# Attention over 4096 tokens: half of the q and k projections moved into the head loop, and context normalised per eight heads

## The reference

```
q, k, v = xn @ q_w.T + q_b, xn @ k_w.T + k_b, xn @ v_w.T + v_b     # 16 heads of 16 columns
attn    = softmax(q @ k.T / 4)                                     # 4096 x 4096 for each head
ctx     = attn @ v ;  attention = ctx @ out_w.T + out_b
ffn     = fp8(xn) @ fp8(weight).T, scaled back, + bias, rounded to bfloat16
```

## Time and profile before

| | us |
|---|---|
| median of 3 runs | 1857.53 (1855.82 to 1859.31) |
| the profiled execution | 1860.13 |
| its span, first to last instruction | 1858.3 |
| ACT busy | 1734.8 (93%), 1912 instructions |
| PE busy | 1639.0 (88%), 33418 matmuls |
| DVE busy | 1637.7 (88%), 1923 instructions |
| POOL busy | 45.9 (2%) |
| DMA, 57.19 MB | 10.3% of 16 engines on the main queue |
| mean granted clock of PE | 0.997 |

### The profile page before, as it was taken

One profiled execution on the slowest core, in us unless ns is written; L12 is line 12 of the kernel. 1 busy time (PEld: TensorE's weight loads), 2 busy tenths in 40 slices (PEclk: granted clock), 3 DMA queues, 4 the chain that ended last, 5 costly groups with the idle time before them and its releaser, 6 DMA issues.

```text
span 1858.3 us, 74491 instructions
## 1 busy us (share of the span) xinstructions
PE 1639.0 (88%) x33418; PEld 553.2 (30%) x33418; DVE 1637.7 (88%) x1923; ACT 1734.8 (93%) x1912; POOL 45.9 (2%) x57
## 2 busy tenths in 40 slices
PE   6998888888888888888888888888888888888888
PEld 4632222222222222222222222222222222222226
DVE  8688989989898998989898998989899898989896
ACT  2379999999999999999999999999999999999990
POOL 0000000000000000000000000000000000000003
PEclk9999999999999999999999999999999999999999
DMA  6430100000010000001010000101000010001003
GB/s 189 163 99 10 32 8 18 20 19 24 10 32 10 24 12 18 24 16 26 10 32 8 16 22 19 24 10 32 10 24 11 18 24 17 26 10 32 8 14 108
DMA packets 94965, 57.19 MB, mean 31 GB/s; under 512 B 55280, under 2 KB 87280, under 8 KB 94640
## 3 DMA queue, kind: packets, MB, share of 16 engines
q1 hardware_dynamic: 94160, 52.18, 10.3%
q10 hardware_dynamic: 480, 0.20, 0.0%
HBM read 30.54 MB, written 17.30 MB: 26 GB/s over the span
## 4 chain that ended last, share of the span: by engine, by line
ACT 44%; issue 31%; PE 15%; DVE 7%; POOL 1%; ACTq 1%; DMA 0%; SPq 0%; POOLq 0%; DVEq 0%
ACT probs L683 44%; PE banks L1312 7%; PE banks L1271 4%; PE banks L1168 3%; DVE bits L988 2%; DVE d_probs L1006 2%; PE banks L1179 1%; DVE o_sb L966 1%; DVE o_junk L967 1%; ACTq L682 1%; POOL o_sb L604 0%; POOL o_junk L604 0%; DMA qk_bias<-in_L_attn_k_b_dram 0%; DVE xn_all L837 0%; PE banks L1152 0%
## 5 line engine op out<-in xcount | busy, mean ns | idle before, releaser
L683 ACT ACTIVATE probs<-banks 128x1024 f32<-128x1024 f32 x1856 | 1701.6, 1165 | 1.7 <-PE banks L1271 1.5
L1312 PE MATMUL banks<-probs,v_st 64*32 64x512 f32 x14848 | 972.2, 590 | 3.6
L1271 PE MATMUL banks<-q_st,k_st 50*32 50x512 f16 x16384 | 782.1, 381 | 193.3 <-ACT probs L683 171.1
L1271 PEld LDWEIGHTS banks<-q_st,k_st 50*32 50x32 f16 x16384 | 230.8, 89 | 1124.1 <-ACT probs L683 1003.2
L1312 PEld LDWEIGHTS banks<-probs,v_st 64*32 64x32 f32 x14848 | 263.3, 106 | 67.9 <-DVE o_junk L967 12.8
L988 DVE TENSOR_SCALAR bits<-banks 128x1024 int32<-128x1024 f32 x192 | 233.9, 1218 | 32.7 <-PE banks L1271 29.4
L995 DVE SCALAR_TENSOR_TENSOR horner<-powers 128x1024 f32<-128x1024 int32 x192 | 235.3, 1226 | 6.6
L1001 DVE SCALAR_TENSOR_TENSOR horner<-powers,horner 128x1024 f32<-128x1024 f32 x192 | 235.2, 1225 | 6.6
L1006 DVE SCALAR_TENSOR_TENSOR d_probs<-horner,bits 128x1024 int32<-128x1024 f32 x192 | 235.2, 1225 | 6.6
L998 DVE SCALAR_TENSOR_TENSOR powers<-powers,horner 128x1024 f32<-128x1024 int32 x192 | 235.1, 1225 | 6.6
L992 DVE TENSOR_SCALAR powers<-bits 128x1024 int32<-128x1024 int32 x192 | 133.2, 694 | 6.6
(11 more groups left out here) (102 smaller groups left out, 418.9 us busy)
## 6 DMA issues: line engine op xcount, KB each, us to landing
k_st<-k_parts SPq DMA_DIRECT2D x102, 64.0 KB, 2.2
q_st<-q_parts SPq DMA_DIRECT2D x198, 32.0 KB, 1.9
k_st<-k_parts SPq DMA_DIRECT2D x102, 60.0 KB, 2.2
q_st<-neg_row SPq DMA_DIRECT2D x264, 1.0 KB, 1.7
xnT_copy<-probs SPq DMA_DIRECT2D x8, 512.0 KB, 3.1
q_parts<-x8T SPq DMA_DIRECT2D x16, 256.0 KB, 2.9
k_parts<-x8T SPq DMA_DIRECT2D x16, 256.0 KB, 2.4
w_f<-xnT_copy SPq DMA_DIRECT2D x16, 256.0 KB, 3.0
```

What stands on the lines that cost most here:

```text
L683: act.activation(probs[:, at:at + WIDE * CHUNK].rearrange("p (t c) -> p t c", t=WIDE), banks[:, bank:bank + WIDE, :], ACT.Exp, bias=EXP_SHIFT,
L1271: last = pe.matmul(banks[cols, bank + g, :], k_st[rows, keys], blocks[rows, j], start=True, stop=True, tile_position=(g * GROUP, t * VCOLS))
L1312: last = pe.matmul(banks[VCOLS * qb:VCOLS * (qb + 1), 6 + half, cols], v_st[keys, kt, :], src[keys, g * CHUNK:(g + 1) * CHUNK][:, cols], s ...
```

## The change

**Ahead of the loop** the second round of projections is gone. The weights for heads 8-15 are copied aside by ACT into `late_w`. SP saves the turned chunk ahead of the parts. The first maximum comes directly behind the last chunk's q and k, and v of the last chunk behind that. Three of the four maxima of x (2048 columns each) go into the first loop; scaling and quantising the ffn weight move to the end of unit 0. A constant headroom now comes out of a filled row of q_st, so that `minus_maxima` has one instruction less.

**Units of heads 0-7** get two additional places (33 and 63 of 67), where PE projects 256 columns of q or k of heads 8-15. DVE takes the result in two instructions (`late_part`), SP saves it in four transfers a unit and loads 256 KB of turned x twice a unit. The places of DVE's blocks and of the maximum differ there: `LATE_D_AT`, `LATE_MAX_AT`.

**Taking sums.** DVE no longer turns and normalises: it adds the two banks into ctx_out by a copy and an addition, and the context is saved as it is. SP also saves the denominators, in four more transfers of 16 pieces of 128 bytes. After eight heads SP loads all their denominators, DVE takes reciprocals of 128x128 numbers for each u, SP saves those and loads them again, each spread over 16 partitions by one of eight transfers. DVE multiplies the context by them in sixteen parts of 128x512 (`scale_context`): parts 0 to 7 in units 17 to 24 (counted from 0; the last unit is 31) behind the block at place 29, parts 8 and 9 behind the last sums, parts 10 to 15 within output groups 0 to 5, each ahead of the group's last addition. SP's loads for 12 to 15 stand between the saves of output groups 0 to 3.

```diff
-    D_AT = (8, 17, 29, 37, 46, 55)
-    MAX_AT = 25
+    D_AT = (8, 17, 29, 37, 46, 55)
+    MAX_AT = 25
+    LATE_D_AT = ((4, 13, 25, 37, 45, 55), (4, 13, 25, 36, 45, 54))
+    LATE_MAX_AT = 21
+    LATE_AT = (33, 63)
+    LATE_UNITS = 16
...
+                self.layouts = [Layout(D_AT)] if full else [
+                    [Layout(LATE_D_AT[u], LATE_MAX_AT, LATE_AT) for u in range(UNITS)],
+                    [Layout(D_AT, MAX_AT) for u in range(UNITS)]]
...
             def save_context(c, h, u):
...
+                    if not c.full:
+                        to = den_dram[k, u, row:row + 1, :].rearrange("o (t x) -> o t x", x=P)[:, :, cols]
+                        sp.dma_start(to, ctx_out[u][qb * VCOLS + DH:qb * VCOLS + DH + 1, :].rearrange(
+                            "v (t x) -> v t x", x=VCOLS)).then_inc(ctx_saved[u], 16)
...
-            save_second(0)
+            for n in range(NCH - 1):
+                save_turned(n)
+                save_parts(n, (0, 1))
             sp.wait_ge(fills, FILLS)
+            sp.wait_ge(parts_saved[buffer_of(1, 0)], SAVED_0 + 32 * (NCH // 2))
             load_k(first, 0, 2)
-            save_second(1)
-            save_second(2)
             load_k(first, 0, 0)
-            save_second(3)
-            save_second(4)
+            save_turned(NCH - 1)
+            save_parts(NCH - 1, (0, 1))
             load_rows(first, 0, 1)
...
+            def share_reciprocals(i):
+
+                k, u, part = i // (UNITS * QB), i // QB % UNITS, i % QB
+                sp.wait_ge(rden_saved, 16 * (k * UNITS + u + 1 if k else UNITS))
+                if i >= 2:
+                    sp.wait_ge(ctx_scaled, i - 1)
+                src = rden_dram[k, u][:, part * CHUNK:(part + 1) * CHUNK]
+                for g in range(HEADS // KD):
+                    sp.dma_start(rden_rows[g * DH:(g + 1) * DH, i % 2, :], src[g, :].partition_broadcast(DH)
+                                 ).then_inc(rden_in[i % 2], 16)
...
                     save_context(c, h, 1)
+                    if not c.full and h == HEADS - 1:
+                        load_dens(1, 1)
+                        for i in scales_loaded(HEADS, 0):
+                            share_reciprocals(i)
...
+                    if not again and i == 0:
+                        save_reciprocals(1, 1)
+                    if not again and i < QB:
+                        share_reciprocals(SCALES - QB + i)
...
+            def scale_context(i):
+
+                k, u, part = i // (UNITS * QB), i // QB % UNITS, i % QB
+                dve.wait_ge(rden_in[i % 2], 16 * (HEADS // KD) * (i // 2 + 1))
+                dve.wait_ge(ctx_saved[u], (k + 1) * (HEADS // KD) * 2 * SAVES)
+                rows = ctxT[:, k, u, part * CT:(part + 1) * CT, :]
+                dve.tensor_tensor(rows, rows, rden_rows[:, i % 2, :].rearrange("p (t x) -> p t x", x=P), ALU.mult
+                                  ).then_inc(ctx_scaled, 1)
...
+                def late_part(h, u, slot):
...
+                    dve.tensor_scalar(buf[:, 0, :], src, qk_bias[:, o, 1:2], None, ALU.add).then_inc(late_hi, 1)
+                    dve.wait_ge(late_hi, i + 1)
+                    dve.scalar_tensor_tensor(out=buf[:, 1, :], in0=src, scalar=qk_bias[:, o, 1:2], in1=buf[:, 0, :],
+                                             op0=ALU.add, op1=ALU.subtract).then_inc(late_ready, 1)
...
-                    chain(dve.transpose(o_sb[:, :], banks[:, 6, :]), link0 + 1)
-                    dve.transpose(o_junk[:, :], banks[:, 7, :]).then_inc(c.acc_free, 1)
...
+                    chain(dve.tensor_copy(o_sb[:, :], banks[:, 6, :]), link0 + 1)
+                    dve.scalar_tensor_tensor(out=ctx_out[u][:, :], in0=banks[:, 7, :], scalar=1.0, in1=o_sb[:, :],
+                                             op0=ALU.mult, op1=ALU.add, accum_out=o_inf[:, span(h * 2 + u, 1)]
+                                             ).then_inc(c.ctx_ready, 1)
...
+                            d_block(h, u, lay.d_at.index(p))
+                            if n == FIRST_SCALED - 1 and p == lay.d_at[1]:
+                                reciprocals(0, 0)
+                                reciprocals(0, 1)
+                            if n == HEADS * UNITS - 1 and p == lay.d_at[2]:
+                                reciprocals(1, 0)
+                            if 0 <= n - FIRST_SCALED < SCALES // KD and p == lay.d_at[2]:
+                                scale_context(n - FIRST_SCALED)
...
+                    if not again and i < GROUPS_OUT - 2:
+                        scale_context(SCALES - GROUPS_OUT + 2 + i)
+                    if not again and i == 0:
+                        reciprocals(1, 1)
                     for b in range(2):
                         dve.wait_ge(proj_done, n * 2 + (b + 1))
...
+                def late_projection(h, u, p, slot):
...
+                    for k in range(KD):
+                        x_cols = late_x[:, slot, k, :]
+                        last = pe.matmul(banks[:, bank_at(h, u, p), 0:LATE_COLS], late_w[:, o, k, :],
+                                         x_cols if o else x_cols.rearrange("f (i j p) -> f j i p", i=CT // 2, j=QB),
+                                         start=(k == 0), stop=(k == KD - 1))
```

More of the change, by code:

```diff
@@ L282, in __init__ @@
[L282 to L286, removed]
-                self.a_index = {p: a for a, p in enumerate(self.a_places)}
-                self.takes = [p for p in range(self.places) if p not in self.a_index]
-                self.head_takes = UNITS * len(self.takes)
@@ L297, in __init__ @@
-                self.sum_at = {kt: at for at, kt in enumerate(self.sum_rows)}
-                self.summed = [1 + max(self.sum_at[kt] for kt in range(half * (KT // 2), (half + 1) * (KT // 2)))
-                               for half in range(2)]
-                left = [(at, None) for at in range(KT)]
-                self.sums_at = {}
-                p = SUMS_FROM
[L304 to L309, removed]
@@ new lines, in __init__, with layout @@
+                self.head_places = UNITS * self.layouts[0].places if full else None
+                self.head_takes = UNITS * len(self.layouts[0].takes) if full else None
+                self.all_takes = HEADS * self.head_takes if full else self.takes_before[-1]
+                lays = self.layouts if full else self.layouts[0] + self.layouts[1]
+                self.summed = [max(lay.summed[half] for lay in lays) for half in range(2)]
+            def layout(self, h, u):
+                if self.full:
+                    return self.layouts[0]
+                return self.layouts[0 if h * UNITS + u < LATE_UNITS else 1][u]
@@ L1258, in scores, with bank_at @@
+                def bank_at(h, u, p):
+                    return WIDE * ((u * c.layout(h, u).places + p if c.full else c.place_0(h, u) + p) % BUFS)
+                def scores(h, u, p):
+                    bank = bank_at(h, u, p)
+                    buffer_free(h, u, p)
+                    kt, j = c.layout(h, u).order[p]
                     blocks = q_st[:, u * UG:(u + 1) * UG].rearrange("k (c j x) -> k j c x", j=QB // GROUPS, x=P)
@@ new lines, in weighted_sum, with sums_of @@
+                    last.then_inc(c.pv_done, 1)
+                def sums_of(h, u, p):
+                    if u:
+                        before = c.layout(h, 0)
+                        for at in before.sums_at.get(p + before.places, ()):
+                            weighted_sum(h, 0, at)
+                    elif not c.full and h:
+                        before = c.layout(h - 1, UNITS - 1)
+                        for at in before.sums_at.get(p + before.places, ()):
+                            weighted_sum(h - 1, UNITS - 1, at)
+                    for at in c.layout(h, u).sums_at.get(p, ()):
+                        weighted_sum(h, u, at)
```

651 lines of the change are left out of this document (392 added, 259 removed).

## The result

| | before | after |
|---|---|---|
| median of the runs | 1857.85 (4 runs, 1855.82 to 1859.31) | 1868.60 (4 runs, 1867.53 to 1869.46) |
| the profiled execution | 1860.13 | 1867.53 |
| its span | 1858.3 | 1865.7 |

The change makes the kernel slower by about 0.6%: the ratio of the times is 1.0058, with a 95% interval of 1.0041 to 1.0076. I had forecast 1858 in a range of 1847 to 1869, and 0.31 for slower. The median lies 0.4 inside the upper end of the range, and the likeliest case, that the terms cancel, did not happen.

The account below looks back on a forecast made before the run. ACT's exponentials bound the kernel, so only prologue, tail and ACT starvation matter. Prologue -19.6, early units +0.2, heads 8-15 +7.7 and tail +12.4 give +0.7 us: 1858 predicted, range 1847 to 1869.

Parts of the forecast that it names:

- the likeliest case: Whole kernel: three large terms cancel within 3.7 us and no change can be told, 1854 to 1861; chance 0.36.
- prologue: Before the first exponential: without the second projection round, first scores at 88.9 instead of 109.5; -19.6 us (-16.5 to -21.5).
- units 2 to 15: Early units of heads 0-7: late places and DVE's new layout cost nothing; 0, bounds 0 to 4.8 for 16 units.
- unit 16: First unit of heads 8-15: two 128x128 reciprocals ahead of place 25 delay the maximum; 1.5 us of stall.
- units 17 to 24: Heads 8-15: DVE's context product ahead of place 37 starves ACT by 0.67 us in each of 8 units; 5.4 us.
- tail: Behind the last exponential: saves, denominators, copies and reciprocals delay group 0 by 10.6, later groups 1.8; loss 12.4 us (9 to 17).
- PE's two matmuls of 256 columns are 0.45 us a place, beside waits for ACT: Late places in units of heads 0-7: PE's projection takes 0.45 us each and fits beside waits for ACT.
- All hold, by 0.3 us: Units of heads 0-7: every DVE block and late part begins before its latest allowed start, by 0.3 us.
- by more than its 0.3 us of margin, say 0.5: 8 us, 1866: Rival, 16 early units: new layout starves ACT beyond DVE's margin; 8 us, 1866; chance 0.31 together with the tail's queue.
- the condition of the rival: Tail: copies through one queue pace six groups if 0.55 us or more each; +8.6, 1867; chance 0.31 with early units slower.
- The marks: Signs: first exponential 89.7, ACT idle 0.6 to 0.7 behind place 37, none in units 1 to 15, copy 0.42 to 0.47, tail 57.
- under 3 or above 14: Whole kernel: total ACT idle time, in us, at which the prediction would count as wrong.

Follow-up runs that it names:

- experiment 3: Changed kernel with the context scaling and unit 16's reciprocals moved behind the last block of their unit; 1863.14 us.
- experiment 4: Changed kernel without the shared copies of reciprocals for parts 10 to 15 and DVE's wait for them; 1863.45 us.
- experiment 6: Changed kernel with scaling and last reciprocals in the output groups moved behind the group's last addition, SP's order unchanged; 1868.23 us.
- experiment 10: experiment 6 with the shared copies for parts 10 to 15 and the save of the last reciprocals issued by ACT instead of SP; 1860.64 us.
- experiment 8: Changed kernel with heads 8-15 normalised as before, scaling behind the last block, and sums behind late places one place later; 1847.17 us, ratio 0.9946 to the kernel before.
- experiments 5: Changed kernel with the weighted sum right behind each late projection (places 34 and 64) moved one place later; 1865.56 us.
- experiment 9: Changed kernel, heads 8-15 normalised as before, scaling behind last block, late projections at 34 and 64, those places' sums one later; 1862.60 us, ratio 1.0032 to kernel before.

## Why the prediction held in its range but not in its sum, point by point

| step | forecast | measured |
|---|---|---|
| prologue | -19.6, with +1 for the clock | -20.97, the clock's cost inside the next line |
| units 0 and 1 | +0.2 | +1.31 |
| units 2 to 15 | 0 (0 to 4.8 for all 16) | +8.76 |
| unit 16 | +1.5 | +1.32 |
| units 17 to 24 | +5.4 | +4.35 |
| unit 31 | +0.8 | +0.65 |
| tail | +12.4 | +12.0 |
| sum | +0.7 | +7.4 |

The range held by 0.4 us, and that is partly luck: the early units left their own bounds (10.1 for 16 units, against 0 to 4.8), while the other terms came out some 3 us better than forecast. The terms for heads 8-15 and the tail were sound.

**The step that failed** is the sentence "PE's two matmuls of 256 columns are 0.45 us a place, beside waits for ACT", and with it "All hold, by 0.3 us". The term was less than half of what it should have been: the projection keeps PE for 1.06 us, 0.61 more. The right number could be had from the earlier trace rows: eight records in 3.60 us are one chunk, and a chunk is four matmuls of 512 columns in the program, so one of them is 0.90, one of 256 columns 0.45 and two 0.90. I divided by the records. The run with half the projection shows both things, two records to a matmul and the loss gone with 0.63 us instead of 1.06. Put into the chain above, 0.45 instead of 1.06 would have the next scores out at 386.25 and 0.63 at 386.43, both before 386.61 (385.69 + 0.917), where that exponential was due; with the true price they end at 386.86.

The Trainium skill ("FP8 and Floating Point Precision", section "TensorE Precision Notes") says that a true FP32 matmul makes four passes through the array. By that an estimate for one projection is 2 matmuls x 4 passes x 256 columns at 2.4 GHz, 0.85 us. The chain's 1.06 and the 36.2 us of the group over 32 projections (1.13) lie above that, and far from the 0.43 that two passes would give by the same estimate. The four records of a projection start 0.32, 0.22 and 0.21 us apart, and by that estimate 0.21 is two passes of 256 columns, so two records to a matmul are four passes and the trace agrees with the page.

The second half of the error was where I looked. I tested whether a place taken by DVE is released in time, three places on. At a late place the buffers were free; PE was late, with scores, sums and a projection between two exponentials. That ACT would be starved in the early units stood among the rivals, "by more than its 0.3 us of margin, say 0.5: 8 us, 1866", and that is what happened in size (10.1 for 16 units). Its reason, DVE's margin, was the wrong one: with DVE's release about 0.5 us earlier nothing moved.

**The prologue** came as worked out: first scores at 88.55 (forecast 88.9), first exponential at 89.30 (89.7). The clock was at 0.50, its 1.2 GHz level, from 89 to 96. In 83 to 89, in which PE was busy for only 0.45 us, it was 0.84 on average, so it had fallen within PE's rest, before the first scores (table of stretches of after; the number ahead of the last two is the clock):

```profile
83.00:89.00 6.00, 0.45 (x16) 0.25 (x24) 2.61 (x3) 0.00 (x0) 1.06 (x3) 0.84 0.13 35
89.00:92.00 3.00, 2.29 (x40) 0.36 (x24) 0.01 (x1) 2.71 (x3) 0.00 (x0) 0.50 0.46 127
92.00:96.00 4.00, 3.51 (x48) 1.15 (x56) 3.90 (x4) 2.95 (x5) 0.00 (x0) 0.50 0.48 142
```

Unit 0 was 0.16 longer than before, with 0.62 of late exponentials in it, so the start at the lower clock cost no more than the dip of before did, where I had put 1.

**Heads 8-15** were right in place and mechanism, shown by moving the work (experiment 3). The price per unit was 0.43 in even units and 0.63 in odd ones (0.75 in unit 17), against 0.67: in even units ACT has some 0.2 us more in hand than the edge I read in an odd one. The reciprocal of 128x128 took 0.94 us where I took 0.8 from the slope between two rows. The repeat count of 8 that the Trainium skill states ("VectorE: DVE Perf Modes", "First, the fixed hardware budget"), read as eight passes an element, gave an estimate of 1.1 and is no better: 0.94 lies between the two, and (0.94 - 0.165) / 127 is 6.1 ns an element, near the slope's 5.9.

**The tail** was right in size: 12.0 against 12.4. The first output addition starts 17.3 us behind the last exponential (1826.29 - 1808.99) instead of 7.85, 9.45 later where I had 10.6; the later groups lose 2.5 where I had 1.8. A copy takes 7.33 / 16 = 0.46 to issue, so the condition of the rival (0.55 or more) was not met. What I had as one chain is two waits on DVE and an order on SP. Without the copies the denominators still hold the first addition to 1824.05 (experiment 4); with DVE's order mended, SP's still holds its save to 1827.45 (experiment 6); with both mended the tail falls (experiment 10).

**The marks.** The first exponential, the place of the wait behind place 37, the copy and the tail came as stated; "none in units 1 to 15" failed, and the idle time at place 40 was 0.33 in even units and 0.52 in odd ones (0.64 in unit 17), mostly under the 0.6 to 0.7 stated. The bound on ACT's idle time, "under 3 or above 14", was badly put: the page's 21.2 lie above it, but 11.6 of them are ahead of the first exponential. The loop itself has 9.6, within the bounds, and yet 16.4 were lost. An exponential that starts late also loses its overlap with its forerunner, and the page counts that as busy (1710.1 against 1701.6). A mark on the length of a unit would have been the right one.

What stays open: the 3.3 us between the medians and the profiled pair, the 0.12 that unit 17 loses beyond the other odd units, and, in the tail, whether the order or the number of SP's transfers is what holds the saves.

## What to carry to other kernels

Price a matmul from the program's count, not from the records of the trace, and check the one against the other; each f32 matmul of a projection here leaves two records. When work goes into a chain in which PE, DVE and ACT pass buffers round, test each engine between two uses of the bound engine, not only the one that holds the buffer. Work on an engine that goes strictly in order can starve the bound engine at one place of the unit and be free at another, as the scaling was. And a new scheme need not be used everywhere: kept to the first eight heads, where its results are not needed at the very end, it spares the tail and keeps the prologue's 21 us. With the sums moved as well (experiment 8) that version is faster than the kernel before by 0.54%.

## What had not been expected of the hardware

How much a late exponential costs follows from its start alone. In the traces of after and of experiments 5 and 9, from unit 2 on, one that starts 0.10 us or more ahead of its forerunner's end ends 0.91 to 0.92 behind that end. With less of a lead it lasts 1.02 to 1.03 and the distance of the two ends grows: 0.08 ahead it is 0.95 (experiment 9), at 0.00 it is 1.02 (9), 0.05 behind 1.07 to 1.08 (after, four in each of units 2 to 15), 1.00 behind 2.03 (9). From these I estimate the cost at 0.107 less the lead. At the late places the idle time shown is only 0.04 to 0.06 of the 0.155 lost; the rest is lost overlap, which the page counts as busy. A start 0.15 ahead, as at place 40 in the earlier trace rows, had cost nothing.
